# One core, eight batches: the planner's durations and table of priorities replaced, the engines' orders built anew

## The reference, cut to what matters

```python
# block 1, "search": LayerNorm, attention with 16 heads of 8, and a second softmax over 8 retrievals
score = softmax(einsum('bihd,bjhd->bhij', q, k))
out = einsum('bhij,bjrd->bihrd', score, v)
comp = softmax(concat([qv, out], -1) @ Ws.T + bs, axis=3)
out = res + lin((comp * out).sum(3), Wf, bf)
x = out + lin(relu(lin(ln(out), Wr1, br1)), Wr2, br2)
...
# block 2, "local": two layers; token shift, qkv, l2norm, rotary, attention in windows of 64 (8 heads of 64)
h = shift_token(x); q, k, v = split(h @ wqkv)
o = local_attention(rotary(l2norm(q)), rotary(l2norm(k)), v)
x = x + o @ wo
h = layernorm(shift_token(x)); a, g = split(h @ w1 + b1)
x = x + (a * gelu(g)) @ w2 + b2
```

## Time and profile before

| what | value |
|---|---|
| median of three runs | 1379.37 us (1377.97 to 1383.18) |
| profiled execution, its own time | 1383.29 us |
| its span from first to last instruction | 1381.5 us |
| mean granted TensorE clock | 0.978 of full |
| PE busy | 1247.4 us, 90% of the span |
| DVE, POOL, ACT busy | 971.1, 901.7, 803.1 us |

### The profile page before, as it was taken

The page is one execution under the profiler, slowest core; times in us unless marked ns, Lnnn a source line. Parts: engine busy times, 40 slices in busy tenths (PEclk is TensorE's granted clock), DMA queues, the critical chain, the costliest instruction groups (busy, mean ns, idle before and its releaser), DMA issues.

```text
span 1381.5 us, 42047 instructions
## 1 busy us (share of the span) xinstructions
PE 1247.4 (90%) x17410; PEld 886.4 (64%) x17410; DVE 971.1 (70%) x1524; ACT 803.1 (58%) x1087; POOL 901.7 (65%) x886
## 2 busy tenths in 40 slices
PE   1689998999999999999999999999999999887885
PEld 1256765666867577666867577675767667565664
DVE  4777489788588876887678776877668673746452
ACT  1256765676656666666656666666656665544442
POOL 4003685778558783878657794778748693979373
PEclk9999999999999999999999999999999999998997
DMA  3410031112101121012111121012201001010100
GB/s 133 157 48 27 11 108 21 25 20 84 41 23 28 47 67 35 19 27 82 43 23 25 42 70 39 18 29 72 52 23 25 10 19 24 17 20 20 32 20 16
DMA packets 112972, 56.70 MB, mean 41 GB/s; under 512 B 82534, under 2 KB 105360, under 8 KB 112784
## 3 DMA queue, kind: packets, MB, share of 16 engines
q1 hardware_dynamic: 108288, 48.52, 13.5%
q10 hardware_dynamic: 4500, 5.51, 1.2%
HBM read 20.18 MB, written 14.68 MB: 25 GB/s over the span
## 4 chain that ended last, share of the span: by engine, by line
PE 77%; POOL 7%; DVE 6%; ACT 5%; issue 3%; DMA 1%; ACTq 1%; SPq 0%; POOLq 0%; DVEq 0%
PE pair L577 66%; PE pair L580 11%; POOL work L1130 3%; DVE gm L1013 2%; POOL rn L1130 2%; ACT probs L775 2%; ACTq L807 1%; ACT L775 1%; DVE o_tok L894 1%; ACT p_t L775 1%; DMA h<-yb 0%; DVE wm L1076 0%; DMA parts_scratch<-shared 0%; ACT work L775 0%; DVE wexp L894 0%
## 5 line engine op out<-in xcount | busy, mean ns | idle before, releaser
L1013 DVE TENSOR_REDUCE gm<-pair 128x2 f32<-128x1024 f32 x256 | 304.2, 1217 | 77.0 <-PE pair L577 74.6
L775 ACT ACTIVATE probs<-pair 128x1024 f32<-128x1024 f32 x256 | 253.8, 1024 | 40.9 <-PE pair L577 28.3
L577 PEld LDWEIGHTS pair<-vt,probs 128*64 128x64 f32 x8192 | 251.0, 138 | 34.5 <-issue 27.5
L577 PE MATMUL pair<-vt,probs 128*64 128x65 f32 x8192 | 268.0, 224 | 0.7 <-ACT gt L775 0.7
L577 PE MATMUL pair<-wqkv,h_t 128*128 128x512 f32 x384 | 188.5, 615 | 3.0 <-ACT h_t L775 1.4
L1130 POOL TENSOR_TENSOR rn<-rn,neg_half 128x16 f32<-128x16 f32 x64 | 187.6, 2932 | 5.3
L1130 POOL TENSOR_TENSOR work<-work 128x1024 f32<-128x1024 f32 (+1 forms) x65 | 151.3, 2328 | 1.0 <-DVE work L894 0.9
L894 DVE TENSOR_TENSOR work<-pair,rot 128x1024 f32<-128x1024 f32 x128 | 150.1, 1214 | 0.0
L775 ACT ACTIVATE raw<-pair 128x260 f32<-128x260 f32 x128 | 49.6, 388 | 142.0 <-PE pair L577 141.9
L1130 POOL TENSOR_TENSOR work<-work,rn 128x1024 f32<-128x1024 f32 x64 | 121.8, 1904 | 4.8
L577 PE MATMUL pair<-h_t,w 128*114 128x256 f32 (+1 forms) x384 | 110.2, 411 | 5.4 <-ACT probs L775 2.0
(11 more groups left out here) (146 smaller groups left out, 2367.4 us busy)
## 6 DMA issues: line engine op xcount, KB each, us to landing
v_mix<-v_nat SPq DMA_DIRECT2D x112, 128.0 KB, 2.8
parts_scratch<-shared SPq DMA_DIRECT2D x16, 384.0 KB, 2.6
k_stack<-parts_scratch SPq DMA_DIRECT2D x64, 96.0 KB, 2.2
q_stack<-parts_scratch SPq DMA_DIRECT2D x64, 96.0 KB, 2.3
parts_scratch<-shared SPq DMA_DIRECT2D x16, 256.0 KB, 2.7
x_in<-in_x SPq DMA_DIRECT2D x8, 256.0 KB, 2.7
parts_scratch<-shared SPq DMA_DIRECT2D x16, 128.0 KB, 2.5
h<-yb SPq DMA_DIRECT2D x64, 32.0 KB
```

The lines of the kernel that those rows point to most:

```text
L577: return pe.matmul(b_out, lhsT, rhs, start=start, stop=stop, skip_group_check=True)
L775: return act.activation(dst, src, fn, **kw)
L1013: m = dve.tensor_reduce(gm[:, g % 2, j, :, s % 2], bank("max", b, s, j), AX, ALU.max, negate=True)
```

## The change

Nothing that is computed changes, nor any instruction's form. Three things that feed `Plan.order` do: the table `TAKEN` is another one; the assumed durations of some parts differ (PE parts in fp32 by 50 to 120 ns more, `max` and `st` 22 to 24 ns less, the two-instruction `*_rstd` of POOL 70 to 100 ns more, `fold` 700 ns less); and of an ACT or DVE part's duration 115 or 90 ns now count as a delay until others see its result, and no more as time in which the engine is taken.

```diff
 TAKEN = {
-    "rem": -9.0, "ma": -8.98, "qk_feat": -8.56, "cos": -8.5, "weight": -8.19, "lsub": -7.11, "qk": -6.98,
...
+    "prod": -9.0, "x_bias": -9.0, "ln1_rstd": -9.0, "lexp": -8.98, "res1b": -8.9, "wf": -8.74, "wsub": -8.4,
...
 }
...
-        self.info[name] = (engine, ns, [a for a in after if a], take, frees, land, table)
+        lag = {"ACT": 115, "DVE": 90}.get(engine, 0)
+        self.info[name] = (engine, ns - lag, [a for a in after if a], take, frees, land + lag, table)
...
-    p.add(("fold", 0), "DVE", 6500, [("low", 0, 0), ("mirror", 0)])
+    p.add(("fold", 0), "DVE", 5800, [("low", 0, 0), ("mirror", 0)])
...
-                add(("pv", b, h), "PE", 1870, [("probs", b, s, j) for j in range(T)]
+                add(("pv", b, h), "PE", 1990, [("probs", b, s, j) for j in range(T)]
```

More of the change, by code:

```diff
@@ L71 @@
 TAKEN = {
-    "rem": -9.0, "ma": -8.98, "qk_feat": -8.56, "cos": -8.5, "weight": -8.19, "lsub": -7.11, "qk": -6.98,
-    "gsplit": -6.93, "sq": -5.78, "qkT": -5.3, "probs": -2.52, "oT": -2.07, "h_turn": -0.17, "max": -0.16,
-    "st": -0.15, "ssq": 0.23, "o": 0.3, "rden": 2.89, "ln4_rstd": 5.72, "sin": 6.23, "ysum": 7.36, "ln1_stats": 7.71,
-    "gturn": 8.23, "out_fold": 8.63, "pv": 8.69, "v_nat": 8.77, "lnl_rstd": 8.85, "attsum": 9.0, "mg": 9.0
+    "prod": -9.0, "x_bias": -9.0, "ln1_rstd": -9.0, "lexp": -8.98, "res1b": -8.9, "wf": -8.74, "wsub": -8.4,
+    "att_turn": -8.4, "h_turn": -8.28, "qkT": -8.14, "gsplit": -7.97, "weight": -4.3, "v_proj": -0.4, "st": -0.39,
+    "max": -0.38, "probs": -0.12, "wo": 0.03, "rnorm": 0.07, "o": 0.23, "mlp2": 0.29, "attsum": 0.38, "gated": 0.78,
+    "ysum": 3.74, "mg": 6.52, "ln4_rstd": 7.46, "m2": 8.86, "sin": 8.89, "m1": 8.98, "pv": 9.0, "ln1_stats": 9.0,
+    "n_feat": 9.0
 }
@@ L264, in plan_search @@
             hf = g // 2
-            add(("rden", b, hf), "DVE", 500, [("raw", b, 8 * hf + k) for k in range(8)])
+            add(("rden", b, hf), "DVE", 630, [("raw", b, 8 * hf + k) for k in range(8)])
             add(("logit", b, hf), "POOL", 1390, [("rden", b, hf), ("v_tok", b), n("lexp", b - 1 + hf, 1 - hf)])
@@ L270, in plan_search @@
             add(("lsum", b, hf), "DVE", 800, [("lexp", b, hf)])
-            add(("weight", b, hf), "POOL", 960, [("lsum", b, hf)])
+            add(("weight", b, hf), "POOL", 930, [("lsum", b, hf)])
             for j in range(T):
@@ L283, in plan_search @@
     add(("ln2_stats", b), "DVE", 1290, [("res1", b), n("ln2_norm", b - 1)])
-    add(("ln2_rstd", b), "POOL", 1360, [("ln2_stats", b)])
+    add(("ln2_rstd", b), "POOL", 1460, [("ln2_stats", b)])
     add(("ln2_norm", b), "POOL", 3130, [("ln2_rstd", b), ("x_turn", b + 1) if b + 1 < batches else None])
     add(("res1b", b), "POOL", 2620, [("ln2_norm", b)])
-    add(("n2_turn", b), "PE", 440, [("ln2_norm", b), n("m2", b - 1)], "one", ("n2_feat", b))
+    add(("n2_turn", b), "PE", 533, [("ln2_norm", b), n("m2", b - 1)], "one", ("n2_feat", b))
     add(("n2_feat", b), "ACT", 780, [("n2_turn", b)])
     for c in range(2):
-        add(("m1", b, c), "PE", 860, [("n2_feat", b)] + ([("spill", b + 1, a) for a in range(2)] if b + 1 < batches else []), "one", ("relu", b, c))
+        add(("m1", b, c), "PE", 933, [("n2_feat", b)] + ([("spill", b + 1, a) for a in range(2)] if b + 1 < batches else []), "one", ("relu", b, c))
         add(("relu", b, c), "ACT", 690, [("m1", b, c)])
@@ L368, in plan_local @@
                 add(("mg", b, l, hf, c), "PE", 430, [("n_feat", b, l, hf)], "one", ("gelu", b, l, hf, c))
-                add(("gelu", b, l, hf, c), "ACT", 470, [("mg", b, l, hf, c)], table="gelu")
+                add(("gelu", b, l, hf, c), "ACT", 485, [("mg", b, l, hf, c)], table="gelu")
             for c in range(3):
```

34 lines of the change are left out of this document (17 added, 17 removed).

## The result

The changed kernel takes 1362.8 us (median of 4 runs, 1361.0 to 1364.1) against 1381.1 for the kernel before on the same chip: ratio 0.986, 95% interval 0.9838 to 0.9882, so 18.3 us less where 7.8 were forecast. The profiled execution took 1360.98 us, its span is 1359.2, against 1383.29 and 1381.5 before.

A forecast was written before the change was run, and what follows sets the result against it. PE bounds the middle, DVE the head, chains through all engines the end; head −2.9, middle +1.0, end −5.9 sum to −7.8 us: 1371.6 us from 1379.4. Own range 1366 to 1377; 8 in 10, 1358 to 1386.

The forecast's parts named there:

- Middle: Five equal full batches, 312.7 to 1099.7 us: −2.9 + 1.6 + 0.8 + 0.7 = +0.2 us per batch, +1.0 in five.
- the more frequent changes of type: Middle, PE's order: bf16/fp32 changes per batch rise from 78 to 98, charged +0.7 us per batch.
- The credit for old waits: Middle: max and st spread singly and qkT further behind qk remove about 2.9 of 4.7 us of PE waits per batch.
- The two charges: Middle, per batch: pv.50 waits for ACT's probs after added table loads, +1.6 us; qkT.310 and gturn for POOL, +0.8.
- the middle wins as well: Rival, chance 0.20: the order absorbs ACT and POOL waits, 2 of 4.7 us per batch left, middle −13, total 1357 us.
- Head: Start up to the second batch, where DVE's score-block reductions hold all else: sum −2.9 us, bounds +1.5 and −6.
- `rem.11`: Head: it moves behind the rowmax parts, taking its waits and work out of the only running chain, −2.4 us.
- `out_fold`: Head: it leaves a hole of DVE and stands ahead of the first rowmax, +1.5 us.
- −0.9 from there to the second batch: Rest of the head: about as many short distances between dependent parts as before, −0.9 us for some pieces out of each other's way.
- End: From 1173.3 us on, one local block left with chains through all engines: five steps sum to −5.9 us, bounds 0 and −10.
- Steps (1) to (3): End, POOL: batch 7's second LayerNorm 1.7 us earlier, third 4.4 with its wait 2.7 shorter, 3.0 left at rnorm.700.
- Steps (4) and (5): End: wo.701 moved ahead of pT.702 and s.703, −0.9; last tile, oT.712 into a wait and wo.713 ahead of mg, −2.0.

The follow-up runs named there:

- p_oon: Kernel before with the new order only from the first part of batch 6's local block on (new end alone): 1378.8 us, ratio 0.9974.
- p_nno: Changed kernel with the old order from the first part of batch 6's local block on (new head and middle): 1369.8 us, ratio 0.9918.
- m_gelu: Changed kernel with one mg and one gelu part per full batch moved up, 44 table loads instead of 54: 1361.9 us, ratio 0.9850.
- m_more: Changed kernel with a one-column exp behind gelu.b010 in the five full batches, two table loads more in each: 1392.7 us, ratio 1.0085.
- m_one: Changed kernel with a 128x1024 copy (about 1.0 us of ACT, no table load) behind gelu.b010 in five full batches: 1368.0 us, ratio 0.9904.
- v_loads: Changed kernel with the last six of ACT's thirteen weight loads issued later, behind raw parts of batch 1: 1362.6 us, ratio 0.9853.

## Why the forecast was off

*Middle, forecast +1.0, measured −10.5 by the traces (five times 2.1) and −7 to −9 by the runs, the seam's clock not counted: here it was wrong.* One of its four terms fits: the more frequent changes of type were put at 0.7 us per batch, and PE's busy time rises by 0.5. That the changes cause this rise was not tested. The credit for old waits was short: 2.9 of 4.7 us were to go, and both of the earlier trace rows and nearly all others went. The two charges stood on differences of two long sums, 9.0 − 7.4 for pv.50 and 16.3 − 14.4 us (less the first wait) for qkT.310. Measured from the end of qk.310 at 703.21, `probs.503` ends after 8.6 us, and PE comes after 9.0, of which 7.8 are work and 1.2 waits. So some wait at this place is there, 1.2 for the 1.6. But it is not the forecast's wait: none of it is for `probs`, 0.9 are for `cos` and `rowmax` on DVE, and the 0.28 for gelu are the most that the two loads can have caused. That the size nearly fits is luck. At qkT.310 PE's work measured 15.1 us instead of 14.4 and POOL's chain 15.9 instead of 16.3 (703.25 to 719.14, PE comes at 719.51): nothing is left of the 0.8. In all the forecast kept 1.8 us of old waits and added 1.6 and 0.8, 4.2; measured are 0.7 (for `o_tok`), 1.2 and 0.2. The step that failed is this: the order of ACT and POOL was read as a danger, and waits of 0.8 to 1.6 us were booked from sums that were themselves off by 0.4 to 0.7 us each, all to the same side. The forecast's own sign of being wrong, a period under 156 us, is met with 155.0.

So the rival "the middle wins as well" came true, with 2 of 4.7 us left as it said. Its 1357 us lie 6 below the median: 1.7 of them since the kernel before measured 1381.1 here and not 1379.4, and the rest since it put the middle at −13, without the rise of PE's busy time (0.5 × 5), and the end at −5.9, while its head of −2.9 was too small.

*Head, forecast −2.9, measured −6.4.* For `rem.11` 2.4 was forecast and 2.8 measured, but this is luck: the chain up to gcopy.00 gained 1.1 us of the 2.36, since PE was not ready either, and 1.8 came from a shorter issue of the weight loads, which no term had. `out_fold` was charged 1.5 and costs nothing by itself. Two signs that the forecast named for the head did not come: the first `rowmax` is at 39.62 instead of 38, and the first `gturn` at 50.39 instead of before 48.5, for the order of PE was left out there. The term that misses most is "−0.9 from there to the second batch", by a count of short distances: the first local layers gained 3.7 us of waits.

*End, forecast −5.9, measured −3.6 by p_oon; the stretches of the profile are 7.1 shorter.* Another 1.3 us, of which the forecast has nothing, lie ahead of it in p_oon: h_turn.600 to h_turn.610 takes 72.3 us there for 73.6. Steps (1) to (3), in relation to h_turn.610. POOL's timeline of the changed kernel, the LayerNorms of batch 7 and rnorm.700:

```profile
1200.51 0.24 POOL L1138 TENSOR_SCALAR rstd<-moments 128x4 f32<-128x4 f32 x1
...
1214.93 0.24 POOL L1138 TENSOR_SCALAR rstd<-moments 128x4 f32<-128x4 f32 x1 [2.93 <-DVE moments L906]
...
1226.83 0.26 POOL L1235 TENSOR_SCALAR rn<-ss 128x16 f32<-128x16 f32 x1
```

The second LayerNorm now waits for nothing (2.99 us before) and starts 42.4 us after h_turn.610 instead of 43.2: −0.8 for −1.7. The third waits 2.93 us instead of 4.89 and starts at 56.8 instead of 59.6: −2.8 for −4.4. rnorm.700 stands at 68.7 instead of 71.2: −2.5 for the −3.0 at the bottom of the chain. Up to there the mechanism was right, with each step smaller than forecast. Of the whole 7.1 us, however, only 0.4 are fewer waits; 6.7 are matmuls that take less time, since the clock in the three stretches is 0.97, 0.94 and 0.88 instead of 0.92, 0.89 and 0.84. And that differs from execution to execution: with the old end the last three stretches take 199.8 to 208.2 us in seven profiles (mean 204.3; p_nno has the 199.8), with the new one 199.4 to 204.5 in eight (mean 201.9). The order's share is about the 2.4 us between the means, of which 1.1 are waits; the two ranges overlap, and the profile of before was the slowest of its seven. With the 1.3 us ahead of h_turn.610 it makes 3.7, and p_oon gained 3.6. So some two thirds of the 7.1 us, which look like more than the forecast's 5.9, are the difference of two executions and not of two orders. Why the clock is lower in one execution of the same order than in another stays open. Steps (4) and (5) can't be told apart from it.

## What to carry to other kernels

Where every engine runs a fixed order, a wait comes from the difference of two chains of 10 us and more. Sums of that length were good to 0.4 to 0.7 us each here, so a difference of 1 us or so was no forecast: it belongs into the range, with zero in it. A term that comes out right can do so for another reason, as `rem.11` did: look at the rows of the chain and not only at the sum. Here the table of priorities and the durations it was found with worked only together; each half alone was slower than no change. And ACT at pv.b00 has no room left: add 1 us and it costs 0.9, add 2.9 and it costs 5.1, since the clock falls behind the longer wait; the two table loads behind it could go or stay. Last, an experiment that takes a cause away has to take it away where the chain needs it; m_gelu's fewer loads said nothing of the two ahead of pv.50.

## What the runs showed of the hardware

A wait of PE of 2.60 us in the middle was followed by matmuls at the lower clock level in all five batches of m_more (3.68 us for 64 that take 2.09 else). Waits up to 0.7 us at the same place left it at the upper one in four of five batches, both in the changed kernel and in m_one, and were followed by the lower one in the fifth.

The clock between 36.0 and 62.7 is given as 0.56 in the changed kernel and as 1.00 in the kernel before. The 1.00 does not fit the matmuls: two matmuls of `max` take 0.61 us there, as they do in the changed kernel where its clock is down, and 0.39 in the middle. PE's timeline of before:

```profile
44.93 0.61 PE L577 MATMUL pair<-k_stack,q_stack 48*128 48x512 bf16 x2 [0.52 <-DVE gm L1013]
```

So PE was at the lower level there in both kernels, and a share of 1.00 at the start of a trace is to be held against the length of a matmul. In this stretch DVE sets the pace: PE waits for `gm` between them, 0.52 us here.

The issue of thirteen loads on ACT takes 9.4 to 11.5 us, of which the second `wqkv` alone 3.49 in the kernel before, against 0.45 for the first; with six fewer of them (v_loads) the other seven take 3.4 us and ACT is free.

A table load costs its own 1.28 us and hardly more. ACT's timeline of m_more:

```profile
720.50 1.28 ACT L778 ACT_TABLE_LOAD   x1
721.80 0.20 ACT L778 ACTIVATE spare<-cols 128x1 f32<-128x1 f32 x1
722.01 1.28 ACT L778 ACT_TABLE_LOAD   x1
723.30 0.47 ACT L778 ACTIVATE gate<-pair,cols 114x256 f32<-114x256 f32 x1
```

The Trainium skill, "ScalarE: Activation LUTs", section "What ACT_TABLE_LOAD costs", counts a drain of 1.38 us besides. Here each load begins within 0.02 us after the instruction ahead of it ends, and no drain shows. From one gelu to the next start it is 3.29 us here and 0.37 in the changed kernel (two take 0.84 together, one 0.47); of the 2.92 more, 0.20 are the added exp, so a load adds 1.36. By the trace the switch costs half of what the skill gives.
